# A weight quantiser split over two stages: pieces of six blocks instead of seven, the last eight blocks moved into later chunks, and one copy moved ahead of an exponential

## The chip, the cores and the metric

The kernel runs on one core of a Trainium2 chip. The metric is the device time of one execution in microseconds (us), from the first to the last instruction and what lies around them. Lower is better. The engines are TensorE (PE, matrix products and transposes), VectorE (DVE), ScalarE (ACT), GpSimd (POOL) and SyncE (SP, which issues transfers). Each runs its own instructions in order and waits on semaphores for the others.

## What is computed

The input is x, 64 sequences of 32 steps and 256 channels, and a condition of 64 x 256. Two layers follow each other:

```python
x = x + L0_attn(L0_cond(cond_2048, x, ...), Wq, Wk, Wv, Wo, gq, gk)          # L0_cond: a GRU over 32 steps
x = x + L0_ffn(L0_cond2(x, cond_2048[:, None, :], b), w_gate, w_up, w_down, ln_weight)   # causal convolution, ternary weights
x = x + L1_attn(L1_cond(x, cond_2048[:, None, :], ...), gamma, Wq, Wkv, Wo)  # small attention, then one with rotary positions
x = x + L1_ffn(L1_cond2(x, cond_2048[:, None, :]), w_fc, w_proj)             # convolution, relu squared
```

The two weights of the last line are quantised in the kernel, in blocks of 64. For each block 16 scales are tried, and the one with the smallest squared error is kept:

```python
base = jnp.maximum(amax, 1e-08) / QMAX              # QMAX = 15, amax over a block of 64
for s in SHRINKS:                                   # 16 factors, 0.4 to 1.0
    scale = base * s
    deq = jnp.clip(jnp.round(wb / scale), -QMAX, QMAX) * scale
    err = jnp.sum((deq - wb) ** 2, axis=-1, keepdims=True)
    # keep the scale of the smallest err
deq = jnp.clip(jnp.round(wb / best_scale), -QMAX, QMAX) * best_scale
```

With 128 partitions each partition holds 64 blocks, 4096 columns in all.

## The kernel before, in words

The order of the work is written by hand for each engine, and semaphores link the engines. It falls into three stages.

**The recurrence** (about 10 to 251 us). A Python loop over 32 steps. In a step PE adds the hidden part of the gates to the input part (L555), does the input part of the next step (L543, L546) and a share of the value projections of earlier states (L573), and turns the new state (L561). ACT takes the tanh of the gates (L1235) and of the candidate (L1239) and copies the turned state (L1245). DVE has five state instructions (L1975 to L1990). The quantiser lies between them. The 64 blocks of a partition are cut into eight pieces of seven blocks (448 columns), one per four steps, and eight blocks are left over. In each step one group of four scales is searched for one piece: ACT makes four scaled copies (`raised`, L1216), cuts the upper two (`from_top`, L1224) and squares (`squares`, L1229, L1230). DVE cuts the lower two (L1957), multiplies and adds four times (L1963, both in `round_off`) and sums the squares per block (L1949, `errors`). Once per piece DVE also finds the maxima (`piece_in`) and chooses and rounds (`piece_out`, spread over four steps), and POOL scales.

**Layer 0** (251 to about 790 us). Eight chunks of 256 tokens. Each chunk has projections, scores, softmax, outputs and, one and two chunks late, the convolution and the feed-forward part. A chunk from 2 on is called a tail chunk, as it also finishes the hidden layer of the chunk two before: `hidden` (L2118, the product of gate and up), `weigh` (L2126), `quantise_hidden` (L2131 to L2143), with ACT's `silu` (L1333) and `hidden_squares` (L1340), and POOL's two powers (L1746, L1750). PE's `gate_up` (L677) writes banks 6 and 7, and waits for `silu` and `hidden` of the previous gate to free them. The eight blocks that are left over are quantised here in chunks 0 and 1: `rest_group` (L1918 to L1923), ACT's `rest_squares` (L1287), `rest_errors` (L1929), `rest_out`. The quantised weights are stored to device memory and come back at the end of layer 0 in eight transfers.

**Layer 1** (about 790 to 1375 us). Nine passes of `chunk1`. A pass does the rotary attention of chunk i, the conditional attention of chunk i + 1 and the feed-forward part of earlier ones. PE turns the quantised weights in passes 0 and 1. Of the rotary part the prediction uses: ACT's exponentials of two halves (`rot_exps`, L1567), PE's outputs per half (`rot_outputs`, L965, four banks), ACT's copies of these (`keep_rot_outputs`, L1574), PE's projection (`rot_project`, L971), and in the conditional part ACT's spread of the probabilities (L1545) for PE's L920.

## Time and profile before

| | us |
|---|---|
| median of 3 runs | 1377.5 |
| lowest, highest | 1376.99, 1380.71 |
| the profiled execution, own time | 1377.21 |
| its span, first to last instruction | 1375.4 |

| engine | busy us | share of the span |
|---|---|---|
| PE, matrix products | 1290.9 | 94% |
| DVE | 1125.6 | 82% |
| ACT | 807.4 | 59% |
| POOL | 86.4 | 6% |

A share of busy time is an average over the three stages, which have different limits. So the rows below are from stretches: the busy time of each engine in a stretch, who waited for whom, and single instructions in order of time. In a timeline a row may join several equal instructions (x8 is eight of them). What stands in square brackets is the idle time of the engine before the row and what ended it. PE's instructions of full precision appear as two records each, and their ends are modelled. The second number behind a line in the busy table is the count of instructions.

### The profile page before, as it was taken

The numbers are of one execution on the slowest core, as the hardware profiler recorded it, in microseconds if no ns is written. First come the engines' busy times: TensorE is split into PE (matmuls) and PEld (weight loads), VectorE is DVE, ScalarE is ACT, GpSimd is POOL, SyncE is SP. The second block draws the span as 40 slices with busy tenths as digits, with TensorE's granted clock in tenths as the row PEclk, the third lists the DMA queues.
The fourth block names the chain that finished last, engine by engine and source line by source line (L and its number), as shares of the span: only waits on it lengthen the run. The fifth ranks groups of instructions, "written<-read, shape, count | busy, mean of one in ns | idle before, by whom it ended". The sixth has DMA issues, their size and how long they took to land.

```text
span 1375.4 us, 25080 instructions
## 1 busy us (share of the span) xinstructions
PE 1290.9 (94%) x9490; PEld 925.9 (67%) x9490; DVE 1125.6 (82%) x2903; ACT 807.4 (59%) x1550; POOL 86.4 (6%) x88
## 2 busy tenths in 40 slices
PE   5999999999999999999999848798999999999988
PEld 2444444578777888878787635476777777787867
DVE  4899999879989686877868889669797988888875
ACT  3999989875555565656565463535454545455323
POOL 0000000101020101010102000000000000000000
PEclk9999999999999999999999979899999999999999
DMA  9432333441111010102030420000000000000000
GB/s 377 123 77 62 77 92 75 151 129 32 40 39 47 32 48 31 48 31 76 3 117 24 157 77 1 24 16 8 9 24 1 24 1 24 1 16 9 8 1 24
DMA packets 26533, 74.18 MB, mean 54 GB/s; under 512 B 3992, under 2 KB 5156, under 8 KB 25136
## 3 DMA queue, kind: packets, MB, share of 16 engines
q1 hardware_dynamic: 25840, 71.62, 16.6%
q8 instruction: 75, 1.23, 0.4%
q10 hardware_dynamic: 576, 0.98, 0.2%
q14 instruction: 42, 0.34, 0.1%
HBM read 49.52 MB, written 23.07 MB: 53 GB/s over the span
## 4 chain that ended last, share of the span: by engine, by line
PE 68%; DVE 25%; ACT 4%; issue 2%; DMA 1%; SPq 0%; DVEq 0%; ACTq 0%
PE psum L619 14%; PE psum L971 9%; PE psum L728 8%; PE psum L940 7%; DVE work L1832 5%; DVE ffn_mem L1949 4%; PE psum L667 4%; PE psum L985 4%; DVE work L1963 3%; PE psum L1013 3%; PE psum L632 2%; PE psum L677 2%; PE psum L886 2%; PE psum L952 2%; PE psum L653 1%
## 5 line engine op out<-in xcount | busy, mean ns | idle before, releaser
L619 PE MATMUL psum<-h_all,w_big 128*128 128x256 f32 x1024 | 241.8, 384 | 1.1 <-ACT work L1283 1.0
L619 PEld LDWEIGHTS psum<-h_all,w_big 128*128 128x128 f32 x1024 | 188.4, 190 | 41.7 <-issue 16.0
L1832 DVE SCALAR_TENSOR_TENSOR work<-work,taps 128x248 f32<-128x248 f32 (+30 forms) x558 | 148.8, 351 | 0.0
L573 PE MATMUL psum<-w_big,h_all 128*64 128x512 f32 x512 | 124.8, 610 | 0.0
L940 PE MATMUL psum<-work,w_big 128*128 128x256 f32 x512 | 118.0, 379 | 0.5 <-DVE gru_mem L2383 0.5
L728 PE MATMUL psum<-w_big,gru_mem 128*128 128x256 f32 x512 | 113.6, 379 | 0.5 <-ACT gru_mem L1325 0.5
L971 PE MATMUL psum<-w_big 128*128 128x256 f32 x448 | 108.2, 393 | 5.9 <-ACT w_big L1574 5.9
L728 PEld LDWEIGHTS psum<-w_big,gru_mem 128*128 128x128 f32 x512 | 96.9, 190 | 14.7 <-ACT gru_mem L1325 0.6
L940 PEld LDWEIGHTS psum<-work,w_big 128*128 128x128 f32 x512 | 96.0, 190 | 13.5 <-DVE gru_mem L2383 0.9
L971 PEld LDWEIGHTS psum<-w_big 128*128 128x128 f32 x448 | 85.4, 195 | 25.8 <-ACT w_big L1574 8.5
L2381 DVE TENSOR_TENSOR gru_mem<-psum,trig 128x256 f32<-128x256 f32 x128 | 54.0, 422 | 40.9 <-PE psum L940 36.9
L1278 ACT ACTIVATE work<-psum,cols 128x512 f32<-128x512 f32 x64 | 44.0, 687 | 65.8 <-PE psum L619 65.8
L573 PEld LDWEIGHTS psum<-w_big,h_all 128*64 128x64 f32 x512 | 50.3, 202 | 42.4 <-issue 35.1
L1283 ACT ACTIVATE work<-psum 128x512 f32<-128x512 f32 x128 | 75.7, 591 | 0.0
L1832 DVE SCALAR_TENSOR_TENSOR h_all<-h_all,taps 128x248 f32<-128x248 f32 (+30 forms) x248 | 67.5, 348 | 0.0
L667 PE MATMUL psum<-probs_t,work 128*128 128x128 f32 x512 | 62.7, 279 | 0.9 <-ACT probs_t L1313 0.9
L667 PEld LDWEIGHTS psum<-probs_t,work 128*128 128x128 f32 x512 | 59.8, 192 | 4.8 <-ACT probs_t L1313 3.5
L2118 DVE SCALAR_TENSOR_TENSOR gru_mem<-psum,stats,work 128x512 f32<-128x512 f32 x28 | 20.9, 748 | 49.2 <-ACT work L1333 46.1
L1593 ACT ACTIVATE h_all<-psum 128x256 f32<-128x256 f32 x64 | 24.5, 383 | 62.4 <-PE psum L985 61.2
L1280 ACT ACTIVATE work<-psum 128x512 f32<-128x512 f32 x64 | 38.2, 597 | 37.3 <-PE psum L619 36.3
L1013 PE MATMUL psum<-ffn_mem,h_all 128*128 128x256 f32 x256 | 58.7, 383 | 0.0
L1013 PEld LDWEIGHTS psum<-ffn_mem,h_all 128*128 128x128 f32 x256 | 47.7, 190 | 12.7 <-issue 6.7
(324 smaller groups left out, 2537.5 us busy)
## 6 DMA issues: line engine op xcount, KB each, us to landing
value_rows<-w_emb SPq DMA_DIRECT2D x128, 128.0 KB, 2.3
work<-value_rows SPq DMA_DIRECT2D x16, 1024.0 KB, 6.0
w_big<-in_Wq SPq DMA_DIRECT2D x2, 2048.0 KB, 16.9
w_big<-in_Wo SPq DMA_DIRECT2D x2, 2048.0 KB, 21.4
out<-w_big SPq DMA_DIRECT2D x15, 256.0 KB, 2.1
x_res<-out SPq DMA_DIRECT2D x15, 256.0 KB, 2.8
w_big<-in_Wv SPq DMA_DIRECT2D x1, 2048.0 KB, 18.6
w_big<-in_Wk SPq DMA_DIRECT2D x1, 2048.0 KB, 23.1
```

The source lines that it names most:

```text
L573: mm = pe.matmul(bank(4 + n)[j * B:(j + 1) * B, :], h_all[:, k, :, 2 * pair + j], w_big[:, 2, k * H * HD + n * 512:k * H * HD + (n + 1) * ...
L619: mm = pe.matmul(bank(n % 2)[:, o * TA:(o + 1) * TA], w_big[:, s, k * H * HD + at:k * H * HD + at + HD], h_all[:, k, bass.ds(i * BA, BA), ...
L667: mm = pe.matmul(bank(4 + n % 2)[:, h * P:(h + 1) * P], v_tok[:, g, e * HD:(e + 1) * HD], probs_t[:, g * HU + e, :], start=True, stop=True)
L728: mm = pe.matmul(wo_out(c, g), o_t[:, h, g * P:(g + 1) * P], w_big[:, 3, h * D:(h + 1) * D], start=(h == 0), stop=(h == H - 1))
L940: mm = pe.matmul(bank((h + 2) % 4)[:, 0:TA], wq1[:, k, h * HD:(h + 1) * HD], xl_t[:, k, :], start=(k == 0), stop=(k == KD - 1))
L971: mm = pe.matmul(bank(wo1_bank(g))[:, 0:D], o1_of(c)[:, h, g * P:(g + 1) * P], wo1[:, h, :], start=(h == 0), stop=(h == H - 1), skip_group ...
L985: mm = pe.matmul(fc_out(c, f), fc_t[:, k, f * P:(f + 1) * P], ffn1(c)[2][:, k, :], start=(k == 0), stop=(k == KD - 1))
L1013: mm = pe.matmul(pj_out(c, g), h2_t[:, f, g * P:(g + 1) * P], proj_t[:, f, :], start=(f == 0), stop=(f == KF - 1))
L1283: act.activation(sq[:, pair % 2 * 2 + s, :], bank(n % 2), ACT.Square).then_inc(proj_kept.sem, 1)
L1832: ins = dve.scalar_tensor_tensor(dst[:, :, lag:], src[:, :, :T - lag], tap, dst[:, :, lag:], ALU.mult, ALU.add)
L1949: dve.tensor_reduce(err[:, g * GROUP:(g + 1) * GROUP, :].rearrange("p s b -> p (s b)"), blocks(w5_tmp[g].rearrange("p j n -> p (j n)")), A ...
L2381: dve.tensor_tensor(by_sequence(q_cos[:, h, :]), src, of_step(cos_q, BA), ALU.mult)
```

## The change

Three edits in one.

1. The pieces hold six blocks (384 columns) instead of seven. Eight pieces are 48 blocks. Sixteen blocks are left over: eight of them go the old way through chunks 0 and 1 (`rest`), the other eight, called `last`, form a new path.
2. The new path. SP loads the eight blocks after the sums for the film rows, into `w_emb`, where they stay: they are not stored and not loaded again. DVE starts them in chunk 2 (`last_begin`), and searches one group at the end of each of chunks 2 to 5 (`last_group`). ACT squares in the next chunk (`last_squares`), and DVE sums there inside `quantise_hidden`, between the maximum and the wait for POOL (`last_errors`). At the end of chunk 6 DVE chooses and rounds (`last_out`).
3. In two rotary passes, 1 and 7, ACT copies the outputs of the first half before it takes the exponential of the second half.

```diff
-PB = 7
+PB = 6
...
-RB = NBLK - PIECES * PB
+RB = (NBLK - PIECES * PB) // 2
 RC = RB * BLK
+LAST_AT = REST_AT + RC
...
+        last = w_emb[:, 2 * D:2 * D + RC]
+        last_abs = w_big[:, 2, 2560:2560 + RC]
+        last_tmp = w_big[:, 2, 0:GROUP * RC].rearrange("p (j n) -> p j n", j=GROUP)
...
             def last_chunk(i):
+                sp.wait_ge(rest_sum.sem, 2 * NG)
...
-                for n in range(PIECES):
+                for n in range(PIECES - 1):
                     sp.dma_start(w5_back[n], w5_dram[:, n * 512:(n + 1) * 512]).then_inc(w5_again, 16)
...
             chunk(0, False, False)
+            sp.wait_ge(film_sum.sem, 1)
+            sp.dma_start(last, io["w5"][:, LAST_AT:]).then_inc(w5_in, 16)
...
-                    pe.wait_ge(w5_again, 16 * PIECES)
+                    pe.wait_ge(w5_again, 16 * (PIECES - 1))
+                    pe.wait_ge(rest_done.sem, 2)
...
+            def last_squares(n):
+                act.wait_ge(rest_set.sem, NG + n + 2)
+                rest_sq.raised_by(act.activation(last_tmp, last_tmp, ACT.Square))
...
                 if tail:
                     hidden_squares(c - 1, 0)
+                    if i > 2:
+                        last_squares(i - 3)
...
+                unfilled = rot and (not late or not cond) and not begun
+                if unfilled:
+                    keep_rot_outputs(i, 0)
                 if rot:
                     rot_exps(i, 1)
...
-                if rot:
+                if rot and not unfilled:
                     keep_rot_outputs(i, 0)
...
+            def last_begin():
+                dve.wait_ge(w5_in, 32)
+                link(dve.tensor_reduce(rest_amax, blocks(last), AX.X, ALU.max, apply_absolute_value=True))
...
+                link(dve.tensor_tensor(blocks(last), blocks(last), per_block(rest_inv), ALU.mult))
+                link(dve.scalar_tensor_tensor(last_abs, last, -1.0, last, ALU.mult, ALU.max))
+
+            def last_group(g):
+                if g:
+                    dve.wait_ge(rest_sum.sem, NG + g)
+                for j in range(GROUP):
+                    ins = dve.tensor_scalar(last_tmp[:, j, :], last_abs, float(1.0 / SHRINKS[g * GROUP + j]), MAGIC,
+                                            ALU.mult, ALU.add)
+                link(ins)
+                link(dve.tensor_scalar(last_tmp, last_tmp, MAGIC + QMAX, MAGIC, ALU.min, ALU.subtract))
+                for j in range(GROUP):
+                    ins = dve.scalar_tensor_tensor(last_tmp[:, j, :], last_abs, -float(1.0 / SHRINKS[g * GROUP + j]),
+                                                   last_tmp[:, j, :], ALU.mult, ALU.add)
+                rest_set.raised_by(ins)
+
+            def last_errors(g):
+                dve.wait_ge(rest_sq.sem, NG + g + 1)
+                rest_sum.raised_by(dve.tensor_reduce(rest_err[:, g * GROUP:(g + 1) * GROUP, :].rearrange("p s b -> p (s b)"),
+                                                     blocks(last_tmp.rearrange("p j n -> p (j n)")), AX.X, ALU.add))
...
                 flink(dve.tensor_reduce(h_max, hid_w, AX.X, ALU.max, apply_absolute_value=True))
+                if meanwhile:
+                    meanwhile()
                 dve.wait_ge(hr_on.sem, GA * c + g + 1)
...
-                    quantise_hidden(c - 1, 0, tail_link)
+                    quantise_hidden(c - 1, 0, tail_link, lambda: last_errors(i - 3) if i > 2 else last_begin())
...
+                if tail:
+                    if i - 2 < NG:
+                        last_group(i - 2)
+                    else:
+                        last_out()
```

`last_out` (not shown) is `rest_out` on the new names, with the final multiplication on DVE instead of POOL: eleven instructions.

How the instructions stand, in three places. First DVE in the recurrence, before, from the last state instruction of a step to the next step's first ones (the names are those of the areas; L1949 sums, L1957 cuts, L1963 multiplies and adds):

```order
L1990 SCALAR_TENSOR_TENSOR gru_mem<-gru_mem,probs_t 128x128
L1949 TENSOR_REDUCE ffn_mem<-work 128x28
L1957 TENSOR_SCALAR work<-work 128x896
L1963 SCALAR_TENSOR_TENSOR work<-probs_t,work 128x448 x4
L1877 TENSOR_TENSOR ffn_mem<-ffn_mem,shrink_tab 128x112
L1879 TENSOR_REDUCE ffn_mem<-ffn_mem 128x7
```

and now:

```order
L2049 SCALAR_TENSOR_TENSOR gru_mem<-gru_mem,probs_t 128x128
L2008 TENSOR_REDUCE ffn_mem<-work 128x24
L2016 TENSOR_SCALAR work<-work 128x768
L2022 SCALAR_TENSOR_TENSOR work<-probs_t,work 128x384 x4
L1894 TENSOR_TENSOR ffn_mem<-ffn_mem,shrink_tab 128x96
L1896 TENSOR_REDUCE ffn_mem<-ffn_mem 128x6
```

The order is the same, and each instruction is a seventh shorter.

Second, DVE from the end of a layer-0 chunk (L2106, the rounded input of the feed-forward part) into the next, at the boundary of chunks 2 and 3, before:

```order
L2106 TENSOR_SCALAR work<-work 128x512
L2118 SCALAR_TENSOR_TENSOR gru_mem<-psum,stats,work 128x512 x2
L2126 TENSOR_TENSOR gru_mem<-gru_mem,ffn_mem 128x1024
L2131 TENSOR_SCALAR stats<-stats 128x1
L2133 TENSOR_REDUCE stats<-gru_mem 128x1
L2136 TENSOR_SCALAR stats<-stats 128x1
```

and now:

```order
L2165 TENSOR_SCALAR work<-work 128x512
L1976 TENSOR_SCALAR w_big<-w_big 128x512 x4
L1979 TENSOR_SCALAR w_big<-w_big 128x2048
L1981 SCALAR_TENSOR_TENSOR w_big<-w_big 128x512 x4
L2177 SCALAR_TENSOR_TENSOR gru_mem<-psum,stats,work 128x512 x2
L2185 TENSOR_TENSOR gru_mem<-gru_mem,ffn_mem 128x1024
L2190 TENSOR_SCALAR stats<-stats 128x1
L2192 TENSOR_REDUCE stats<-gru_mem 128x1
L1987 TENSOR_REDUCE v<-w_big 128x32
L2197 TENSOR_SCALAR stats<-stats 128x1
```

The group (L1976 to L1981) stands before the first hidden product, and the error sum (L1987) between the maximum and the scalar instruction that waits for POOL.

Third, ACT in the last rotary pass, before (the two exponentials L1567, both halves' copies L1574, then the turned rows L1581 and the feed-forward part):

```order
L1595 ACTIVATE h_all<-h_all 128x256
L1567 ACTIVATE work<-work 128x512 x2
L1574 ACTIVATE w_big<-psum 128x16x32 x8
L1581 ACTIVATE work<-psum 128x512
L1593 ACTIVATE h_all<-psum 128x256
```

and now:

```order
L1609 ACTIVATE h_all<-h_all 128x256
L1581 ACTIVATE work<-work 128x512
L1588 ACTIVATE w_big<-psum 128x16x32 x4
L1581 ACTIVATE work<-work 128x512
L1588 ACTIVATE w_big<-psum 128x16x32 x4
L1595 ACTIVATE work<-psum 128x512
```

The first four copies moved ahead of the second exponential.

## Rows read from the trace of the kernel before

**Rows 1.** Busy time by stretch (length, then busy us by engine): recurrence, chunk.

```profile
54.06:248.60 194.54, 180.85 (x877) 80.33 (x875) 183.34 (x372) 175.81 (x316) 12.31 (x13) 1.00 0.33 78
520.20:585.30 65.10, 65.10 (x648) 52.44 (x641) 50.74 (x134) 38.28 (x66) 6.48 (x3) 1.00 0.13 41
```

**Rows 2.** Waits, 54 to 248 us: who, for whom, total us, times, longest.

```profile
PE psum L561 <- DVE gru_mem L1990: 13.6, 25, 0.9
```

**Rows 3.** Timeline of PE, recurrence: start us, length us, line, instruction, idle before.

```profile
32.96 0.33 PE L561 MATMUL psum<-ident,gru_mem 128*128 128x128 f32 x1
39.91 0.33 PE L561 MATMUL psum<-ident,gru_mem 128*128 128x128 f32 x1
...
54.20 0.33 PE L561 MATMUL psum<-ident,gru_mem 128*128 128x128 f32 x1
...
243.33 0.33 PE L561 MATMUL psum<-ident,gru_mem 128*128 128x128 f32 x1 [0.95 <-DVE gru_mem L1990]
250.76 0.48 PE L561 MATMUL psum<-ident,gru_mem 128*128 128x128 f32 x1 [2.16 <-DVE gru_mem L1990]
```

**Rows 4.** DVE lines of the quantiser: ns min/median/max, first and last start us.

```profile
L1949 DVE TENSOR_REDUCE ffn_mem<-work x24: 2009/2010/2014, 39.6 to 265.7; 128x28 f32<-128x1792 f32 x24
L1929 DVE TENSOR_REDUCE v<-w_big x4: 2276/2276/2287, 295.7 to 338.4; 128x32 f32<-128x2048 f32 x4
L1963 DVE SCALAR_TENSOR_TENSOR work<-probs_t,work x48: 617/619/627, 56.6 to 257.1; 128x448 f32<-128x448 f32 x48
L1923 DVE SCALAR_TENSOR_TENSOR w_big<-work,w_big x16: 684/685/693, 281.8 to 330.1; 128x512 f32<-128x512 f32 x16
L1957 DVE TENSOR_SCALAR work<-work x24: 615/617/621, 24.8 to 253.4; 128x896 f32<-128x896 f32 x24
```

**Rows 5.** ACT's pass over the upper half of a group, the same view.

```profile
L1224 ACT ACTIVATE work<-work,top_col x24: 1027/1033/1058, 21.5 to 254.3; 128x896 f32<-128x896 f32 x24
```

**Rows 6.** Timeline of DVE: a group's first instruction, and the one behind it.

```profile
279.08 1.43 DVE L1918 TENSOR_SCALAR w_big<-work 128x512 f32<-128x512 f32 x4
284.22 0.18 DVE L1838 TENSOR_SCALAR stats<-stats 128x32 int32<-128x32 int32 x1
```

**Rows 7.** Timeline of DVE in a layer-0 chunk, from its first hidden product.

```profile
586.90 0.75 DVE L2118 SCALAR_TENSOR_TENSOR gru_mem<-psum,stats,work 128x512 f32<-128x512 f32 x1 [5.69 <-ACT work L1333]
595.40 0.21 DVE L2136 TENSOR_SCALAR stats<-stats 128x1 f32<-128x1 f32 x1 [2.18 <-POOL stats L1750]
613.65 0.74 DVE L1828 TENSOR_SCALAR work<-work,taps,cols 128x256 f32<-128x256 f32 x2 [1.02 <-ACT work L1350]
```

**Rows 8.** ACT: end of that chunk's hidden squares; line L1287 by itself.

```profile
591.71 0.18 ACT L1340 ACTIVATION_READ_ACCUMULATOR gru_mem<-gru_mem 128x1 f32 x1
L1287 ACT ACTIVATE w_big<-w_big x4: 1902/1910/1912, 286.1 to 330.8; 128x2048 f32<-128x2048 f32 x4
```

**Rows 9.** Timeline of the same chunk: DVE's third product, PE's fourth gate.

```profile
597.62 0.75 DVE L2118 SCALAR_TENSOR_TENSOR gru_mem<-psum,stats,work 128x512 f32<-128x512 f32 x1
598.48 1.03 PE L677 MATMUL psum<-ffn_mem,work 128*128 128x512 bf16 x4
```

**Rows 10.** Timeline of the same chunk: POOL's power and DVE's L2126.

```profile
589.36 5.43 POOL L1746 TENSOR_TENSOR stats<-stats,minus_half 128x32 f32<-128x32 f32 x1 [44.65 <-ACT stats L1301]
590.75 1.22 DVE L2126 TENSOR_TENSOR gru_mem<-gru_mem,ffn_mem 128x1024 f32<-128x1024 f32 x1
```

**Rows 11.** Timeline of PE and ACT in the last rotary chunk.

```profile
1317.66 1.64 PE L965 MATMUL psum<-work,v 32*128 32x512 f32 x8
1322.24 5.41 PE L971 MATMUL psum<-w_big 128*128 128x256 f32 x16 [2.93 <-ACT w_big L1574]
1320.15 2.04 ACT L1574 ACTIVATE w_big<-psum 128x512 f32<-128x512 f32 x4
```

**Rows 12.** Timeline of ACT and PE in rotary chunk 1.

```profile
945.56 2.54 ACT L1545 ACTIVATE probs_t<-work 32x512 f32<-32x512 f32 x4 [2.89 <-DVE work L2348]
949.13 1.08 PE L920 MATMUL psum<-probs_t,work 128*32 128x128 f32 x32
```

More of the change, by code:

```diff
@@ L497, in _ @@
             chunk(0, False, False)
+            sp.wait_ge(film_sum.sem, 1)
+            sp.dma_start(last, io["w5"][:, LAST_AT:]).then_inc(w5_in, 16)
             chunk(1, False, True)
             sp.wait_ge(rest_done.sem, 1)
-            sp.dma_start(w5_dram[:, REST_AT:], rest).then_inc(w5_out, 16)
-            with sp.Fori(0, NA - 3) as last:
-                chunk(last + 2, True, True)
+            sp.dma_start(w5_dram[:, REST_AT:LAST_AT], rest).then_inc(w5_out, 16)
+            with sp.Fori(0, NA - 3) as later:
+                chunk(later + 2, True, True)
             last_chunk(NA - 1)
@@ L1737, in _ @@
             pool.wait_ge(in_step.sem, in_step.at(PIECES + 1, 0))
-            rest_based.raised_by(pool.tensor_tensor(blocks(rest), blocks(w5[:, REST_AT:]), per_block(rest_inv), ALU.mult))
+            rest_based.raised_by(pool.tensor_tensor(blocks(rest), blocks(w5[:, REST_AT:LAST_AT]), per_block(rest_inv), ALU.mult))
             times_scale(PIECES - 2)
@@ L1788, in _ @@
             rest_done.raised_by(pool.tensor_tensor(blocks(rest), blocks(rest), per_block(rest_scale), ALU.mult))
-            with pool.Fori(0, NA - 3) as last:
-                chunk(last + 2, True, True)
+            with pool.Fori(0, NA - 3) as later:
+                chunk(later + 2, True, True)
             head_rms(UNITS - 2)
@@ L1900, in slink @@
                     link(ins, in_step, PIECES)
-                slink(dve.tensor_reduce(rest_amax, blocks(w5[:, REST_AT:]), AX.X, ALU.max, apply_absolute_value=True))
+                slink(dve.tensor_reduce(rest_amax, blocks(w5[:, REST_AT:LAST_AT]), AX.X, ALU.max, apply_absolute_value=True))
                 slink(dve.tensor_scalar(rest_base, rest_amax, 1e-8, None, ALU.max))
@@ L1944, in rest_out @@
                 rest_set.raised_by(dve.tensor_scalar(rest, rest, MAGIC, MAGIC, ALU.add, ALU.subtract))
+            def last_begin():
+                dve.wait_ge(w5_in, 32)
+                link(dve.tensor_reduce(rest_amax, blocks(last), AX.X, ALU.max, apply_absolute_value=True))
+                link(dve.tensor_scalar(rest_base, rest_amax, 1e-8, None, ALU.max))
+                link(dve.tensor_scalar(rest_base, rest_base, 1.0 / QMAX, None, ALU.mult))
+                link(dve.reciprocal(rest_inv, rest_base))
+                link(dve.tensor_tensor(blocks(last), blocks(last), per_block(rest_inv), ALU.mult))
+                link(dve.scalar_tensor_tensor(last_abs, last, -1.0, last, ALU.mult, ALU.max))
@@ new lines, in last_errors, with last_out @@
+            def last_errors(g):
+                dve.wait_ge(rest_sq.sem, NG + g + 1)
+                rest_sum.raised_by(dve.tensor_reduce(rest_err[:, g * GROUP:(g + 1) * GROUP, :].rearrange("p s b -> p (s b)"),
+                                                     blocks(last_tmp.rearrange("p j n -> p (j n)")), AX.X, ALU.add))
+            def last_out():
+                dve.wait_ge(rest_sum.sem, 2 * NG)
+                link(dve.tensor_tensor(rest_err, rest_err, shrinks_sq.unsqueeze(2).broadcast_to([P, NS, RB]), ALU.mult))
+                link(dve.tensor_reduce(rest_best, rest_err.rearrange("p s b -> p b s"), AX.X, ALU.min))
+                link(dve.tensor_tensor(rest_pick, rest_err, rest_best.unsqueeze(1).broadcast_to([P, NS, RB]), ALU.is_gt))
+                link(dve.scalar_tensor_tensor(rest_pick, rest_pick, 2.0, shrinks.unsqueeze(2).broadcast_to([P, NS, RB]),
+                                              ALU.mult, ALU.add))
+                link(dve.tensor_reduce(rest_shr, rest_pick.rearrange("p s b -> p b s"), AX.X, ALU.min))
+                link(dve.reciprocal(rest_ishr, rest_shr))
+                link(dve.tensor_tensor(rest_scale, rest_shr, rest_base, ALU.mult))
+                link(dve.tensor_tensor(blocks(last), blocks(last), per_block(rest_ishr), ALU.mult))
+                link(dve.tensor_scalar(last, last, float(QMAX), -float(QMAX), ALU.min, ALU.max))
+                link(dve.tensor_scalar(last, last, MAGIC, MAGIC, ALU.add, ALU.subtract))
+                rest_done.raised_by(dve.tensor_tensor(blocks(last), blocks(last), per_block(rest_scale), ALU.mult))
@@ L2126, in weigh, with quantise_hidden @@
                 dve.tensor_tensor(hid_w, hid, ln_row, ALU.mult).then_inc(hidw_on.sem, 1)
-            def quantise_hidden(c, g, flink):
+            def quantise_hidden(c, g, flink, meanwhile=None):
                 _, hid_w, hid_q, _, _ = hid_bufs(c)
```

2 lines of the change are left out of this document (1 added, 1 removed).

## The prediction, made before the changed kernel was run

> **What bounds the kernel now.** I read the page first, then the busy table of two stretches, as the page's shares are averages over stages. The table splits them: in the recurrence (54 to 249 us) PE, DVE and ACT are all near 90% or more, DVE highest with 183.34 of 194.54 us; in a layer-0 chunk (65.1 us) PE is busy 65.10 of 65.10 us and DVE only 50.74 [rows 1]. So the two places want opposite things: DVE work is dear in the recurrence and has 14.4 us of room in a chunk. What counts there is where the room lies.
>
> Third view, the waits of the recurrence: PE stood before the turn of the new state (L561) for 13.6 us in 25 times, each time for the last DVE instruction of the step, L1990 [rows 2]. The starts of L561 in the timeline give the pitch: from 54.20 to 243.33 us are 25 steps, 189.13 us, 7.565 us each. The same PE work ran from 32.96 to 39.91 us without a wait: 6.95 us [rows 3]. DVE sets the pitch, but PE is only 0.6 us per step behind it.
>
> **The quantiser's pieces.** Each of the 32 steps holds one group of the search. Its DVE part loses 64 of 448 columns in every instruction. The costs come from the same operations at two widths [rows 4]: the error sum took 2010 ns for 1792 columns and 2276 for 2048, 1.04 ns per column, so 256 fewer columns save 0.265 us. The four multiply-adds took 619 ns at 448 and 685 at 512, 66 ns per 64 columns, so 4 x 66 = 0.26 us. The cut-off (617 ns at 896) runs at about twice that rate: 128 columns, 0.07 us. The work on a piece (maximum, final rounding, once in four steps) has five 448-wide instructions, 65 or 33 ns less each, about 0.06 us per step. The sum is 0.65 us: DVE alone would allow 7.565 - 0.65 = 6.91 us.
>
> ACT loses work too. At 0.76 ns per column (1910 ns at 2048 [rows 8] against 1033 at 896 [rows 5]) four raised copies save 4 x 49 ns and three 896-wide passes 3 x 97 ns: 0.49 us, from 175.81 / 194.54 x 7.565 = 6.84 us busy per step [rows 1] to 6.35. ACT does not become the limit.
>
> What is late next is PE. Its bound of 6.95 us sits 0.04 above DVE's 6.91. DVE's steps are unequal (243.33 to 250.76 is 7.43, the mean 7.565 [rows 3]), but it can run ahead in a short step, as nothing but the state ties it to PE, so the long step is absorbed. The gain is 25 x (7.565 - 6.95) = 15.4 us if the clean step repeats, and 13.6 us if only the waits go [rows 2, 3]. I take 14.5. After the last step PE waits 2.16 us [rows 3]; it issues less there, and its DVE path shortens by the same 0.65 us: 0.8 with the lead that DVE then has (bounds 0 and 2.16). Start-up and hand-over to the projections hold some ACT-bound waits of the same copies; from some 0.4 us less ACT work in one step I estimate 0.7 for both ends together (bounds 0 and 2). Part a: -16.0 us.
>
> The transfer of the input weights is 256 KB shorter at the start and comes later as a load of its own; the store and the reload of the eight last blocks go. All lie beside computation: SP has nothing urgent behind the new wait for the film sums, since it stands after the value load that needs later outputs, and the wait in the last chunk is met early in chunk 6.
>
> **The eight blocks in chunks 2 to 6.** Three additions per chunk.
>
> A group of the search goes to the end of chunks 2 to 5. The same group for the first eight blocks ran from 279.08 to 284.22 us: 5.14 us [rows 6]. It falls into the idle stretch before the first hidden product, 5.69 us long, ended by ACT L1333 [rows 7]. 0.55 us remain: cost 0. If this cover were gone, its length would stand in full before L2118, whose product frees the bank that PE's next gate needs. The final choice in chunk 6 has eleven instructions: four 512 wide, of at most 0.69 us each as L1923 [rows 4], and seven on 128 columns or fewer, at most 0.4 us by estimate. That is under 5.6 us, in the same gap: 0.
>
> The error sum goes between the maximum and the wait for POOL, 2.18 us of idle [rows 7]. It needs ACT's square. ACT is free at 591.9 us (its accumulator read starts at 591.71 and lasts 0.18), and the square of 2048 columns took 1910 ns for the first eight blocks [rows 8]: done at 593.8. DVE's sum of 2.28 us then ends near 595.95, and L2136 begins there and not at 595.40: +0.55 us. Queued behind it on DVE is the third hidden product, L2118 at 597.62 for 0.75 us, then ending at 598.9. PE starts gate 3 at 598.48 [rows 9] and needs that bank about 0.43 us later, for its second half: a wait of 0 to 0.15 us. The rest of the chain is absorbed before the convolution, where DVE idles 1.0 us [rows 7]. Chunk 2 has instead the beginning (three instructions of 512 columns, some 0.69 us each, and three small ones, 0.2 by estimate), 2.7 us in the 2.18 us gap: +0.5 us, within the same slack. I take +0.3 us for all five chunks; bounds 0 and 5 x 0.55 = 2.75.
>
> The trace shows POOL's power running from 589.36 for 5.43 us, and DVE's two-operand L2126 starting inside it at 590.75 and lasting 1.22 us for 1024 columns [rows 10], just what L1963 and L1923 give without POOL (1.03 ns per column and 0.16 fixed, 1.21 us [rows 4]). So the two-operand instructions of the beginning should not wait for POOL. The Trainium skill (SBUF — State Buffer, "Summary: rules for kernel authors") speaks against that: a DVE operation with two SBUF inputs and a GpSimd one that reads SBUF exclude each other, and the second waits. By that rule the beginning would end about 0.8 us later, and part b would be 1.1 instead of 0.3; the row disagrees, so the sum goes by the row.
>
> **The rotary copies.** In the last rotary chunk PE starts the outputs at 1317.66 us; the copies run from 1320.15 for 2.04 us, behind the second exponential, and PE waits 2.93 us for them until 1322.24. Put first, they can start when the first output is done. I take 1.15 us after its start, 1318.8, within bounds of 0.3 and 1.64 (the length of the PE row): copies done at 1320.85, and PE goes on 1.3 us earlier (0.9 to 2.2). The exponential is then about 1.2 us later; what needs it, PE's second outputs, comes only after PE's projection of 5.41 us, with over 3 us of room [rows 11].
>
> In chunk 1 the same exchange starts PE's projection about 0.9 us earlier, but the exponential slips behind the copies, by 1.5 us (estimated from the 1.2 of the last pass, where DVE's scores are ready later), and with it the DVE chain to ACT's spread of the conditional probabilities (945.56, 2.54 us long). That then ends at 949.6; PE wants it at about 948.2 and began at 949.13 before [rows 12]. Net +0.5 us (bounds -0.9 and +1.5). Part c: -1.3 + 0.5 = -0.8 us.
>
> **The sum** against the profiled execution, 1377.2 us (its span is 1375.4): -16.0 + 0.3 - 0.8 = -16.5, so 1360.7. The median of the runs is 0.3 above that execution: 1361.0 us.
>
> **Rivals.**
> 1. PE's true floor is higher. The three engines hand the state around, and with PE, DVE and ACT within 0.7 us of each other each wait of one falls on the next. For it: DVE's 6.91 and PE's 6.95 almost meet, and some steps have 0.5 us more ACT or DVE work. Against it: the loop of the state alone is much shorter than the pitch. If half of part a's 14.5 us stays, the time is 1361.0 + 7.2 = 1368.2 us.
> 2. The DVE work of the chunks reaches PE. The added work is 4 x 5.14 + 4 x 2.28 + 2.7 + some 4.5 (the final choice) = 36.9 us. PE has no idle in a chunk [rows 1], so every microsecond by which DVE delays a bank is lost. The place is L2118: if the group and the sum come in front of it by a full delay, the price is 36.9 us, 0.3 of it in the sum already, and the time 1361.0 + 36.6 = 1397.6 us. It turns the gain of 16.8 us into a loss once 46% of the added work is uncovered. Against it: by length, all but 1 us per chunk has a gap.
> 3. DVE is no limit in the recurrence after all, so that the change doesn't do there what it says, and only part c and the ends are left: 1375 us. Rows 2 name DVE 25 times, so little speaks for it.
>
> **Chances.** Forecast (1357 to 1365): 0.66. Rival 1 (1365 to 1372): 0.22. Rival 2: 0.06, of which 0.04 end slower than 1381.6 and 0.02 in between. Rival 3: 0.03, within the bound in half of it and just beyond in the other. A gain above the sum (PE's pitch below 6.95, or more at the ends), under 1357: 0.03. The measurement of this kernel tells 0.3%, 4.1 us, from no change. Faster: 0.66 + 0.22 + 0.03 + half of rival 3 and a little of rival 2 = 0.93; same 0.03; slower 0.04. The range 1357 to 1370 leaves out rivals 2 and 3, the 0.03 below and about 0.05 of rival 1: 0.17.
>
> **What the changed profile would show.** L561 at a pitch of 6.95 to 7.02 us with waits of under 0.1 us, DVE with waits before L1975 or for ACT instead. DVE's idle before the first hidden product down from 5.69 to about 0.5 us; the error sum starting about 3.0 us after its chunk's first L1340 and PE's row of a chunk still 65.1 us. In the last rotary chunk a PE wait of 1.6 instead of 2.93 us. The forecast is wrong if the pitch is above 7.15 or if a chunk lasts over 65.6 us.

## The result

| | before | after |
|---|---|---|
| median, us | 1378.01 (4 runs, 1376.99 to 1380.71) | 1361.33 (4 runs, 1359.24 to 1362.78) |
| span of the profiled execution | 1375.4 | 1359.6 |

The ratio is 0.9875, 95% interval 0.9855 to 0.9894. The prediction was 1361.0.

The lines named here moved down by 7 to 61: L561 is now L568 (the state's turn), L555 L562, L573 L580, L677 L684, L965 and L971 are L972 and L978, L1574 is L1588, L1545 L1559, L1949 L2008, L1957 L2016, L1963 L2022, L2118 L2177, L2136 L2197. L1224 is L1232.

**The recurrence.** Busy time by stretch, as in [rows 1]: the 25 steps from 54.16 us, and one layer-0 chunk.

```profile
54.16:228.40 174.24, 174.10 (x853) 77.90 (x851) 160.87 (x364) 158.11 (x307) 11.00 (x13) 1.00 0.34 81
504.30:569.50 65.20, 65.20 (x641) 52.42 (x640) 57.99 (x145) 40.07 (x67) 6.48 (x3) 1.00 0.14 42
```

PE is busy for the whole of the recurrence's stretch, and DVE is below it. In the chunk DVE went from 50.74 to 57.99 us, and PE stays full. PE's waits for the state, 54 to 237 us, against the 25 of [rows 2]:

```profile
PE psum L568 <- DVE gru_mem L2049: 1.5, 1, 1.5
```

The timeline of PE at the turns, answering to [rows 3]:

```profile
54.30 0.33 PE L568 MATMUL psum<-ident,gru_mem 128*128 128x128 f32 x1
...
228.30 0.33 PE L568 MATMUL psum<-ident,gru_mem 128*128 128x128 f32 x1
235.05 0.33 PE L568 MATMUL psum<-ident,gru_mem 128*128 128x128 f32 x1 [1.48 <-DVE gru_mem L2049]
```

From 54.30 to 228.30 us are 25 steps of 6.96 us, with no wait at the turn. The only wait left stands before the last turn. The DVE and ACT lines at the new widths, against [rows 4, 5]:

```profile
L2008 DVE TENSOR_REDUCE ffn_mem<-work x24: 1741/1745/1754, 39.6 to 248.4; 128x24 f32<-128x1536 f32 x24
L2022 DVE SCALAR_TENSOR_TENSOR work<-probs_t,work x48: 550/552/560, 56.1 to 240.6; 128x384 f32<-128x384 f32 x48
L2016 DVE TENSOR_SCALAR work<-work x24: 548/550/555, 23.9 to 237.4; 128x768 f32<-128x768 f32 x24
L1232 ACT ACTIVATE work<-work,top_col x24: 919/923/937, 20.7 to 238.2; 128x768 f32<-128x768 f32 x24
```

**A layer-0 chunk.** DVE and PE in chunk 3, against [rows 7 to 9]:

```profile
440.55 0.75 DVE L2177 SCALAR_TENSOR_TENSOR gru_mem<-psum,stats,work 128x512 f32<-128x512 f32 x1 [0.55 <-ACT work L1345]
447.45 2.29 DVE L1987 TENSOR_REDUCE v<-w_big 128x32 f32<-128x2048 f32 x1 [0.58 <-ACT w_big L1299]
449.66 0.20 DVE L2197 TENSOR_SCALAR stats<-stats 128x1 f32<-128x1 f32 x1
```

```profile
452.13 1.14 PE L684 MATMUL psum<-ffn_mem,work 128*128 128x512 bf16 x4
```

The gap of 5.69 us is filled down to 0.55. DVE waits 0.58 us for the square (L1299), and the scalar instruction behind the error sum starts 0.6 us late (0.61 against the kernel before, with the rows of PE laid on each other). PE's row of four gate products at 452.13 takes 1.14 us where 1.03 is usual: 0.1 us is what reaches it.

**The last rotary pass**, PE and ACT, against [rows 11]:

```profile
1304.43 1.64 PE L972 MATMUL psum<-work,v 32*128 32x512 f32 x8
1307.77 3.72 PE L978 MATMUL psum<-w_big 128*128 128x256 f32 x16 [1.70 <-ACT w_big L1588]
```

```profile
1305.65 2.06 ACT L1588 ACTIVATE w_big<-psum 128x512 f32<-128x512 f32 x4 [3.83 <-PE psum L972]
```

The wait is 1.70 us instead of 2.93, and the projection behind it takes 3.72 us instead of 5.41.

**Where the 15.8 us of the two spans are.** The same row of PE was found in both traces, and its times subtracted. The stretches between those in the table differ by under 0.1 us.

| stretch | after less before, us | predicted |
|---|---|---|
| start-up, to the turn at 54.20 | +0.10 | |
| 25 steps | -15.13 | -14.5 |
| last step | -0.68 | -0.8 |
| hand-over to layer 0 | -0.62 | -0.7, start-up included |
| chunks 2 to 6 | +0.61 | +0.3 |
| layer 1, pass 0 | +1.87 | 0 |
| pass 1 | +0.62 | +0.5 |
| last pass and end | -2.58 | -1.3 |

The 1.87 us of pass 0 were in no term. PE's first projection there, before and after:

```profile
882.29 3.72 PE L971 MATMUL psum<-w_big,gru_mem 128*128 128x256 f32 x16
```

```profile
866.69 5.48 PE L978 MATMUL psum<-w_big,gru_mem 128*128 128x256 f32 x16
```

Sixteen equal records, 3.72 and 5.48 us. Two more stretches of the table hold the clock. From the first turn of the state to the sixth (54.20 us in the kernel before) the first profile took 36.81 us, against 36.18 before, but at a mean granted clock of 0.91 against 0.95. And in the kernel before the last turn took 0.48 us where 0.33 is usual [rows 3]: the mean granted clock from there to 254 us was 0.50, and the changed kernel's profile has 1.00 behind its last turn. Both come up again below. So the experiments had three things to settle: what bounds the recurrence now, what the path of the last eight blocks costs, and what the clock does in layer 1.

### The profile page after: what moved, and what is told of

It reads as the page before. It is cut to its first block, busy times and chain, and to the rows that moved or that the text cites. A ratio compares the mean times of both kernels' runs of the same rounds, so it can differ in the third digit from the quotient of the medians.

```text
span 1359.6 us, 25143 instructions
## 1 busy us (share of the span) xinstructions
PE 1288.5 (95%) x9490; PEld 926.3 (68%) x9490; DVE 1139.4 (84%) x2960; ACT 798.7 (59%) x1554; POOL 85.0 (6%) x88
## 3 DMA queue, kind: packets, MB, share of 16 engines
q8 instruction: 75, 1.23, 0.4%
## 4 chain that ended last, share of the span: by engine, by line
PE 80%; DVE 14%; ACT 3%; issue 1%; DMA 1%; SPq 0%; DVEq 0%; ACTq 0%
PE psum L626 14%; PE psum L735 8%; PE psum L580 7%; PE psum L978 7%; PE psum L947 7%; DVE work L1849 5%; PE psum L674 4%; PE psum L992 4%; PE psum L1020 3%; PE psum L553 3%; PE psum L562 3%; PE psum L639 2%; PE psum L684 2%; PE psum L893 2%; PE psum L959 2%
## 5 line engine op out<-in xcount | busy, mean ns | idle before, releaser
L580 PE MATMUL psum<-w_big,h_all 128*64 128x512 f32 x512 | 124.0, 606 | 0.0
L978 PE MATMUL psum<-w_big 128*128 128x256 f32 x448 | 106.5, 389 | 3.8 <-ACT w_big L1588 3.8
L978 PEld LDWEIGHTS psum<-w_big 128*128 128x128 f32 x448 | 84.4, 193 | 23.0 <-ACT w_big L1588 6.4
L580 PEld LDWEIGHTS psum<-w_big,h_all 128*64 128x64 f32 x512 | 50.3, 203 | 42.7 <-issue 35.5
L1763 POOL TENSOR_TENSOR stats<-stats,minus_half 128x32 f32<-128x32 f32 x7 | 38.4, 5482 | 280.9 <-ACT stats L1313 280.9
```

The source lines that it names most:

```text
L580: mm = pe.matmul(bank(4 + n)[j * B:(j + 1) * B, :], h_all[:, k, :, 2 * pair + j], w_big[:, 2, k * H * HD + n * 512:k * H * HD + (n + 1) * ...
L978: mm = pe.matmul(bank(wo1_bank(g))[:, 0:D], o1_of(c)[:, h, g * P:(g + 1) * P], wo1[:, h, :], start=(h == 0), stop=(h == H - 1), skip_group ...
```

## The experiments

Experiments 1 to 4 ran beside a kernel before of 1380.2 us, 5 to 8 beside 1378.66, 9 to 12 beside 1378.46, so ratios are compared, not times. Experiments 9 and 10 have one execution each (1355.57 and 1352.48 us), so only their rows are read. Where an interval is some 0.4% wide, a difference of 1 or 2 us is read in the trace, from the same rows of PE.

### 1 to 3: the rotary copies

1: `unfilled = False`. 2: `unfilled = rot and not cond and not begun`. 3: the third edit alone, on the kernel before.

> The changed kernel with its third edit undone: both rotary passes take the second exponential ahead of the first copies again. Theory A (the clock is part of it; read from the two traces): in the last pass the edit took 1.23 us off PE's wait and the projection behind it ran in 3.72 instead of 5.41 us, as the granted clock did not fall; pass 1 lost 0.62. Undoing it costs +2.58 - 0.62 = +2.0 us: 1363.3, and the last pass's projection takes 5.41 us again. Theory B (the prediction's term c, waits only): +0.8 us, 1362.1, and 5.41 against 3.72 us is chance, so that the projection may take 3.72 us here as well.

> The changed kernel with the early copies in the last pass alone; pass 1 as before the change. Theory A: pass 1 gives its 0.62 us back (no PE wait of 1.41 us for the spread of the conditional probabilities), the last pass keeps its 2.58: 1360.7 us. Rival: the projection of pass 1 starts 0.85 us later and the gain is lost there, the spread being late either way: 1361.3 to 1361.6.

> The kernel before with the third edit alone. If the parts add up: 1378.0 - 2.0 = 1376.0 us, with PE's wait in the last pass 1.70 us and the projection behind it 3.72 us (the clock is kept). By waits alone: 1377.2, projection 5.41 us.

Measured: 1366.19 us, ratio 0.9883 (0.9864 to 0.9902); 1363.01 us, 0.9865 (0.9844 to 0.9886); 1378.98 us, 0.9987 (0.9976 to 0.9998). Timeline of PE in the last pass, first experiment 1 (copies late), then 2 (copies early):

```profile
1310.18 6.71 PE L978 MATMUL psum<-w_big 128*128 128x256 f32 x16 [2.94 <-ACT w_big L1588]
```

```profile
1308.02 5.41 PE L978 MATMUL psum<-w_big 128*128 128x256 f32 x16 [1.69 <-ACT w_big L1588]
```

The ratios are too near each other to tell the theories apart: that of experiment 3 is 1.8 us below its kernel before, where 2.0 and 0.8 were expected, with an interval of 0.3 to 3.3. So the rows decide. Waits went as expected (2.94 and 1.69 us). The projection did not: 6.71 us in 1, and 5.41 in 2 although its copies are early. Experiment 3 had 3.72 us in the last pass (2.93 us gained up to the end of the projection, 0.35 of it lost again behind it) but in pass 1 this:

```profile
942.84 3.72 PE L971 MATMUL psum<-w_big 128*128 128x256 f32 x16 [2.08 <-ACT w_big L1574]
950.73 1.42 PE L920 MATMUL psum<-probs_t,work 128*32 128x128 f32 x32 [3.10 <-ACT probs_t L1545]
952.08 5.02 PE L971 MATMUL psum<-w_big 128*128 128x256 f32 x16
```

The projection (942.84) ran fast there, but PE then stood 3.10 us for the spread, and the next two rows ran slowly: pass 1 lost 2.26 us in all, and not 0.6. Neither theory holds: the time behind a wait isn't fixed.

### 4: without the new path

```diff
-                    if i > 2:
-                        last_squares(i - 3)
-                    quantise_hidden(c - 1, 0, tail_link, lambda: last_errors(i - 3) if i > 2 else last_begin())
+                    quantise_hidden(c - 1, 0, tail_link)
-                if tail:
-                    if i - 2 < NG:
-                        last_group(i - 2)
-                    else:
-                        last_out()
```

> The changed kernel without the new path: the eight last blocks are loaded but not quantised (that part of the computation is left out). What chunks 2 to 6 pay for it: by the landmarks of the two traces 0.1 us per chunk and 0.2 in chunk 2, 0.6 us in all: 1360.7. The prediction's term was 0.3: 1361.0. Rival (contention or bank delays that the landmarks hide, or the low clock in pass 0 of layer 1 being a consequence of the path's waits there): 2 us or more, 1359.3 or less, with pass 0 at the speed of before (projection of pass 0 3.72 instead of 5.48 us).

Measured: 1361.06 us, 0.9861 (0.9841 to 0.9882). Against the changed kernel's first profile its rows of PE stand at +0.25 us after chunk 1 and at -0.38 after chunk 6: the path costs 0.63 us, 0.2 in chunk 2 and 0.11 in each of the others. The rival falls: pass 0's projection took 3.72 us here, but also in experiments 5, 6, 8, 9, 11 and 12, which have the path.

### 5, 9 and 10: what bounds the recurrence

5: one multiply-add of four left out (`for j in range(1, GROUP)` in `round_off`). 9: in every second tile of the values the product of the second half of the channels is left out. 10: both.

> The changed kernel with three instead of four multiply-adds per group of the search in the recurrence (one of four is left out of the computation): 0.55 us less DVE work per step, DVE alone would allow about 6.4 us. Theory (PE sets the pitch): the pitch stays at 6.95 to 6.96 us, the time within 1 us of 1361.3. Rival 1 of the prediction (the engines hand the state around and each wait of one falls on the next): the pitch falls by 0.2 us or more, 5 us or more in the time.

> The last try left out one of a pair of products whose two halves of 64 columns share a time slot, so PE lost next to nothing (the step's row of four records went from 1.14 to 1.12 us and the one behind it from 1.46 to 1.86). Here both halves of the pair go: four records fewer per step, about 1.0 us (part of the values isn't computed). Only the pitch of the recurrence is read. PE alone would allow about 5.97 us. By the prediction's count DVE binds at 6.91 us: pitch 6.90 to 6.95. Rival: DVE had more room than counted: pitch below 6.85.

> The same with one multiply-add of each group left out on DVE as well. DVE's count is then 6.91 - 0.55 = 6.36 us, PE's 5.97, ACT's 6.35 (busy time of before less the prediction's 0.49). If the three bounds stand for themselves, the pitch is 6.36 to 6.45 us. Rival 1 of the prediction (waits of one engine fall on the next): 6.6 us or more.

The turns 25 steps apart, in experiments 5, 9 and 10 in this order:

```profile
53.73 0.33 PE L568 MATMUL psum<-ident,gru_mem 128*128 128x128 f32 x1
...
227.53 0.33 PE L568 MATMUL psum<-ident,gru_mem 128*128 128x128 f32 x1
```

```profile
52.19 0.33 PE L568 MATMUL psum<-ident,gru_mem 128*128 128x128 f32 x1
...
224.52 0.33 PE L568 MATMUL psum<-ident,gru_mem 128*128 128x128 f32 x1 [0.63 <-DVE gru_mem L2049]
```

```profile
52.48 0.33 PE L568 MATMUL psum<-ident,gru_mem 128*128 128x128 f32 x1
...
220.42 0.33 PE L568 MATMUL psum<-ident,gru_mem 128*128 128x128 f32 x1
```

5: 6.95 us per step (1360.22 us, ratio 0.9864, 0.9847 to 0.9881). Less DVE work brings nothing: PE is the bound. 9: 6.89 us per step. PE was busy for 154.07 of 170 us (55 to 225 us), 6.25 us per step, so its work fell by 0.7 us, and the pitch by 0.06 only. PE's idle time is 11.5 us behind the turn, for ACT's copy of the turned state (L1253), and 3.9 us ahead of it, for DVE. So without DVE PE would step at about 6.73 us, and DVE holds it at 6.89; the prediction's count for DVE was 6.91. 10: 6.72 us, where 6.36 to 6.45 were expected of three bounds that stand for themselves. Busy time of 10, 55 to 225 us, in the columns of the first table, then PE's waits there, and PE's timeline from one turn to the next:

```profile
55.00:225.00 170.00, 156.72 (x762) 68.84 (x761) 150.93 (x344) 160.20 (x310) 11.00 (x13) 1.00 0.36 86
```

```profile
PE psum L562 <- ACT h_all L1253: 12.0, 25, 0.5
PE psum L568 <- DVE gru_mem L2049: 1.3, 6, 0.2
```

```profile
106.25 0.33 PE L568 MATMUL psum<-ident,gru_mem 128*128 128x128 f32 x1
107.06 1.57 PE L562 MATMUL psum<-gru_mem,h_all 128*64 128x384 f32 x8 [0.47 <-ACT h_all L1253]
...
112.89 0.33 PE L568 MATMUL psum<-ident,gru_mem 128*128 128x128 f32 x1
```

ACT is busy 94% of the time, PE 92%, DVE 89%, and none is full. But PE's 156.72 us of work and its two waits, 12.0 and 1.3 us, make up the whole 170 us: PE still sets the pitch. The products that were left out are those that PE does between the turn (L568) and the first product that needs its copy (L562). They had covered ACT's copy, and without them PE stands 0.47 us for it in every step. So the edit took 0.7 us of work off PE and gave 0.47 us back as a wait, and PE's own bound in 9 and 10 is about 6.7 us and not 5.97. That explains the 0.3 us between the expectation and 6.72; DVE delays PE by 0.05 us per step. What experiment 10 can't tell is whether the pitch would have come down to DVE's 6.36 us with a faster PE. In the changed kernel PE has no such wait.

### 6 and 7: an experiment that missed

In every second tile one product of 64 output columns was left out: 6 from the changed kernel, 7 from the kernel before.

> The changed kernel with one of the eight value products of a step left out of the recurrence (part of the values isn't computed): 0.46 us less PE work per step. PE alone would allow 6.49 us. By the prediction's count DVE then binds at 6.91 us, so the pitch falls by only 0.04 us and the time by 1 us. Rival: DVE's bound is lower than counted, or there is none, and the pitch falls towards 6.5 us, 11 us in all.

> The kernel before with the same value product left out: PE 0.46 us less per step. Theory (DVE set the pitch before): pitch 7.57 us and time 1378.0 unchanged, PE's waits longer by 0.46 us each. Rival 3 of the prediction (DVE was no limit): pitch 7.1 us, time 1366.

Measured: 1368.1 us, 0.9927 (0.9902 to 0.9953), and 1386.22 us, 1.0058 (1.0037 to 1.0079). The pitch hardly moved in either (6.94 and 7.56 us), which says nothing, as PE's work hardly fell. PE in experiment 6, one step:

```profile
102.73 0.33 PE L568 MATMUL psum<-ident,gru_mem 128*128 128x128 f32 x1
102.99 1.13 PE L580 MATMUL psum<-w_big,h_all 128*64 128x512 f32 x2
103.54 1.86 PE L562 MATMUL psum<-gru_mem,h_all 128*64 128x384 f32 x8
```

The same two rows in the changed kernel:

```profile
103.22 1.15 PE L580 MATMUL psum<-w_big,h_all 128*64 128x512 f32 x4
104.20 1.46 PE L562 MATMUL psum<-gru_mem,h_all 128*64 128x384 f32 x8
```

The four hidden products (L562) take 1.86 us behind two records where they took 1.46 behind four, and end 2.4 us behind the first record in both. The two halves of 64 columns run beside each other, so half a pair saves nothing. The Trainium skill says that the array can be split into tiles that are independent of each other (TensorEngine Tiling (Array Packing), "Overview"); these rows agree. Both kernels lost some 7 us elsewhere, in chunks 2 to 6. PE's waits of experiment 6 there, 300 to 760 us:

```profile
PE psum L626 <- issue: 2.4, 2, 1.9
PE psum L660 <- issue: 2.3, 4, 0.8
```

The changed kernel has no wait of this kind there. "Issue" means that nothing in the profile held PE. The program of PE is 30 instructions shorter ahead of these places; experiment 9, with 60 fewer, has no such loss. Why it comes is open.

### 8: the group without its gap

```diff
                     quantise_hidden(c - 1, 0, tail_link, lambda: last_errors(i - 3) if i > 2 else last_begin())
+                    if i - 2 < NG:
+                        last_group(i - 2)
...
-                if tail:
-                    if i - 2 < NG:
-                        last_group(i - 2)
-                    else:
-                        last_out()
+                if tail and i - 2 >= NG:
+                    last_out()
```

> The changed kernel with the group of the search moved from the end of its chunk to behind the error sum's place in the hidden quantiser of the same chunk, ahead of the third hidden product: 5.14 us of DVE work without a gap, the same count of instructions. Theory (the prediction's cover, rival 2's price): each of four chunks pays 5.14 less about 0.4 us of slack, 4.7 us; 1361.3 + 19 = 1380 us. Rival (the place doesn't matter, as DVE has 14 us of room in a chunk and catches up): under 3 us, 1364 or less.

Measured: 1390.33 us, 1.0086 (1.0068 to 1.0104): 29 us slower than the changed kernel. By the rows of PE the four chunks lost 7.65, 7.15, 6.73 and 6.62 us, more than the 5.14 us that the group lasts. PE in chunk 3, then the second of the two rows in the changed kernel, then the busy table of that row's stretch:

```profile
463.97 1.03 PE L684 MATMUL psum<-ffn_mem,work 128*128 128x512 bf16 x2 [5.07 <-DVE gru_mem L2177]
464.79 8.62 PE L735 MATMUL psum<-w_big,gru_mem 128*128 128x256 f32 x32
```

```profile
442.63 7.07 PE L735 MATMUL psum<-w_big,gru_mem 128*128 128x256 f32 x32
```

```profile
464.79:473.25 8.46, 8.46 (x34) 7.09 (x32) 8.14 (x13) 2.98 (x4) 0.00 (x0) 0.82 0.00 0
```

PE waited 5.07 us for the hidden product, and the 32 records behind it took 8.62 us instead of 7.07, at a mean granted clock of 0.82 instead of 1.00. So this wait of 5.07 us cost 1.5 us more than itself in the row behind it alone.

### 11: the changed kernel again

> The changed kernel again, unaltered. Theory (TensorE's granted clock behind short waits in layer 1 differs from execution to execution): pass 0's projection, 5.48 us in the first profile, may take 3.72 us as in six of the nine other profiles, and pass 1 and the last pass may differ as well; time 1359 to 1364 us. Rival (each kernel has its own fixed pattern): 5.48, 5.41 and 3.72 us in passes 0, 1 and 7 again.

Measured: 1360.83 us, 0.9881 (0.9865 to 0.9898). PE in passes 0 and 1:

```profile
865.92 3.72 PE L978 MATMUL psum<-w_big,gru_mem 128*128 128x256 f32 x16
...
925.49 3.72 PE L978 MATMUL psum<-w_big 128*128 128x256 f32 x16 [2.08 <-ACT w_big L1588]
933.38 1.60 PE L927 MATMUL psum<-probs_t,work 128*32 128x128 f32 x32 [3.10 <-ACT probs_t L1559]
934.91 4.84 PE L978 MATMUL psum<-w_big 128*128 128x256 f32 x16
```

The same program, and pass 0's projection takes 3.72 us and not 5.48. In pass 1 the projection ran fast and the rows behind the wait slowly. The rival falls. (The expectation counts six fast ones among the nine other profiles; they were seven.) All fourteen profiles, by the length of the first projection (16 records):

| pass | copies | full clock, 3.72 us | lower clock |
|---|---|---|---|
| 0 | not edited | 10: before, 3 to 9, 11, 12 | 4: after, 1, 2, 10 (5.48 to 5.80) |
| 1 | late, wait 2.93 | none | 5: before, 1, 2, 7, 12 (5.23 to 5.41) |
| 1 | early, wait 2.08 | 7: 3, 4, 5, 6, 8, 9, 11 | 2: after, 10 (5.41) |
| last | late, wait 2.93 | none | 3: before, 1, 7 (5.37 to 6.71) |
| last | early, wait 1.70 | 9: after, 3 to 6, 8 to 11 | 2: 2, 12 (5.41) |

Behind a wait of 2.93 us the clock was at its lower level in all eight cases, behind one of 2.08 in two of nine, behind one of 1.70 in two of eleven. Where it held behind the 2.08 us of pass 1 it was low behind the next wait, of 3.10 us, in all seven cases. What decides between the two the rows do not show.

### 12: a candidate

```diff
-                rest_sq.raised_by(act.activation(last_tmp, last_tmp, ACT.Square))
+                for h in range(2):
+                    part = last_tmp[:, 2 * h:2 * h + 2, :]
+                    rest_sq.raised_by(act.activation(part, part, ACT.Square))
```

The error sum is cut in the same way, and `unfilled` is that of experiment 2.

> A candidate: the changed kernel with the early copies in the last pass alone, and with the square and the error sum of the last eight blocks cut in two halves of 1024 columns each, so that DVE sums the first while ACT squares the second. Theory: the second half's sum ends about 0.1 us before POOL's power and the 0.1 us per chunk vanishes in chunks 3 to 6 (-0.4 us); pass 1 gives back 0.6 to 0.8 us: 1.1 us below the unaltered changed kernel of the same call. That is less than the measurement tells; the landmarks of the trace must show it. Rival: the halves cost as much as they save (two fixed costs), and the chunk stays 0.1 us longer.

Measured: 1359.61 us, 0.9865 (0.9849 to 0.9882), 1.2 us below the changed kernel that ran beside it (experiment 11), which the intervals do not tell apart. DVE and then PE in chunk 3:

```profile
446.58 2.35 DVE L1991 TENSOR_REDUCE v<-w_big 128x16 f32<-128x1024 f32 x2
448.85 0.20 DVE L2202 TENSOR_SCALAR stats<-stats 128x1 f32<-128x1 f32 x1
```

```profile
451.81 1.03 PE L684 MATMUL psum<-ffn_mem,work 128*128 128x512 bf16 x4
```

DVE sums without a wait, and the scalar instruction starts at 448.85 us, 0.48 us earlier than in the changed kernel once the 0.33 is taken off by which this execution is ahead. PE's row is back at 1.03 us. Over chunks 3 to 6 PE gains 0.43 us, as expected: the halves hold. Pass 1, from the start of the outputs to the conditional projection, takes 15.16 us, against 15.79 in the first profile of the changed kernel and 17.42 in experiment 11. But the last pass's projection ran at the lower clock (5.41 us), as in experiment 2, which gives 1.69 us back. Another 1.47 us went in chunk 7, where this execution has the lower clock (0.50 from 754 to 757 us) and the changed kernel's two profiles do not. Both kernels with the early copies in the last pass alone had the slow projection there, and none of the nine profiles with them in both passes. Whether that is chance is open.

## Why the prediction was right

**The recurrence** carried the forecast and held. The unit costs came out: the error sum 1745 ns (2010 less 265 predicted, exactly that), each multiply-add 552 (619 less 66 is 553), the cut 550 (617 less 67 is 550). ACT's pass fell by 110 ns where 97 were counted: that is 0.86 ns per column, and the 0.76 of the prediction came from two different operations. PE's floor, read from one clean step of before, was the pitch of 25 steps (6.96 us), and experiments 5 and 9 show that the two bounds lie where the count put them: PE at 6.95, DVE at 6.89 against 6.91. I had taken 14.5 between 13.6 and 15.4; 15.13 is near the upper end, so the cautious discount of 0.9 us was not needed. Rival 3 is excluded as far as the pitch goes: it fell by 0.61 us with the work of DVE and ACT. That it was DVE's share is read from the waits and not from a run, as experiment 7 missed: in the kernel before PE and ACT stood 13.6 and 18.2 us for DVE in the 25 steps, and DVE 4.9 us for ACT. Rival 1 is excluded for this kernel: PE has no wait in the 25 steps, and less work on DVE changed nothing (experiment 5). Experiment 10 was to look for it further down and met another limit, a wait that its own edit uncovered. The last step gave 0.68 of the 0.8.

**Start-up and hand-over** were sized at 0.7 us together, and the first profile shows 0.52. At equal clocks it is more. The turn of 54.30 us stood between 52.78 and 54.59 in seven executions of kernels that are the same up to there. From the first turn to the sixth five of them took 35.35 to 35.63 us, at a mean granted clock of 0.95, and two (the first profile and experiment 12) 36.81 and 36.90 us at 0.91; the kernel before and experiment 3, with the old recurrence, took 36.18 and 36.10 us at 0.95. So the narrower pieces save 0.5 to 0.8 us there, which the first profile hid behind the clock. Of the 0.62 us of the hand-over 0.14 are the clock: experiment 3, without the lower level there, took 6.46 us from the last turn to the seventeenth record of L619, and the kernel before 6.60. The term was too small, and that it fits the profile is luck.

**The eight blocks.** The gap carried the group in all four chunks at no cost that shows, and experiment 8 shows what the gap was worth: 7 us per chunk. Rival 2's mechanism was right, its price too low, as the clock adds to each wait. The delay of L2136 by 0.55 us was seen (0.6), and what reached PE, bounded by 0 and 0.15 us, was 0.10 to 0.11 in chunks 3 to 6; 0.2 in chunk 2. The total was 0.61 to 0.63 instead of the 0.3 taken: I had set the middle of the bounds too low. In chunk 2 stands the beginning: its two-operand instructions on DVE, and POOL's two powers beside them:

```profile
382.99 0.69 DVE L1969 TENSOR_TENSOR w_emb<-w_emb,stats 128x512 f32<-128x512 f32 x1
383.72 0.69 DVE L1970 SCALAR_TENSOR_TENSOR w_big<-w_emb 128x512 f32<-128x512 f32 x1
377.72 5.43 POOL L1763 TENSOR_TENSOR stats<-stats,minus_half 128x32 f32<-128x32 f32 x1 [0.49 <-ACT stats L1313]
383.11 0.97 POOL L1767 TENSOR_TENSOR stats<-stats,minus_half 128x1 f32<-128x1 f32 x1
```

DVE's two take the length that they have without POOL (685 ns in [rows 4]). POOL's second power, which starts while the first of them runs, takes 0.97 us, as in all ten profiles that have the beginning (0.97 to 0.98); in the other chunks it takes 0.54, and in experiment 4, without the beginning, 0.55 in chunk 2 too. DVE's scalar instruction starts at 384.44 us behind L1970 in any case, so PE loses nothing by it. So the rule of the Trainium skill that the prediction weighed (SBUF — State Buffer, "Summary: rules for kernel authors") shows here after all, though on POOL's side: the second to start waits, 0.43 us. The prediction's row was the long power, under which DVE runs on freely, and it does so here as well (L2185, with two operands, starts inside it at 379.11 us and takes 1.23 us); what was concluded for DVE held, and of a wait on POOL's side the prediction had nothing.

**The rotary copies** hold in the term of the wait (-1.23 predicted as -1.3, copies 1.22 us behind the start of the outputs, 1.15 taken). What the prediction missed is the clock: in [rows 11] it had the row L971 with 5.41 us, and 3.72 is what sixteen such records take at the full clock. The busy table of that row, before and after:

```profile
1322.24:1327.58 5.34, 5.34 (x17) 4.11 (x17) 5.34 (x17) 0.00 (x0) 0.00 (x0) 0.68 0.00 0
```

```profile
1307.77:1311.42 3.65, 3.65 (x16) 2.96 (x17) 3.06 (x7) 0.46 (x1) 0.00 (x0) 1.00 0.00 0
```

0.68 and 1.00. So in this execution the row behind the shorter wait took 1.69 us less as well, and 0.35 was lost at the end. 1.00 is the level of 2.4 GHz, and 0.68 is a mean over stretches at it and at 1.2 GHz; before both rows PE had waited, 2.93 and 1.70 us. The Trainium skill describes these two levels, the lower one after idle time (TensorE: Matmul & The Clock Gate, "What's actually happening"); the rows agree in direction, and the table of experiment 11 shows that the same wait can go either way. In pass 1 the net price was 0.62 us as predicted (0.5), but only because pass 1's projection was slow in that profile; in seven of nine it was not, and the price was then about 2.3 us. So the agreement of this term is luck.

**The offset.** The mechanisms were right, but that the total is right to 0.3 us is in part luck, as its errors cancel. The last pass gave 1.28 us more than was counted, for the clock, and the 25 steps 0.63 us more; pass 0 took 1.87 us, for the clock too, and the other terms together some 0.7 us. That leaves 0.7 us, and the median of the runs lies 0.1 below the profiled execution, where 0.3 above was taken. The 1.87 us are no fixed effect of the change: the same program was without them in experiment 11. Whether the change makes them more frequent is open (4 of 11 profiles with the new recurrence had them, none of 3 with the old one).

## What to carry to other kernels

Find the second bound before moving work off the first: here DVE had 0.65 us per step to lose and only 0.61 of it counted, because PE's clean step (one pair of rows without a wait) was 6.95 us. Work moved into a gap costs what the gap's end delays, and the same work outside the gap can cost more than its length, as the clock was lower behind PE's longer wait (experiment 8). Before work is left out to find a bound, look what it covers: behind the turn it was a copy on another engine, and 0.47 us of the 0.7 came back as a wait (experiments 9 and 10). When a PE row behind a wait is longer than the same records elsewhere, shortening the wait may give back that difference too, but not in every execution, so don't count it as certain.

## What was not expected of the hardware

- The granted clock behind the same wait differs between executions of one program: 5.48 or 3.72 us for sixteen records of pass 0 (0.67 and 1.00 of full speed).
- POOL's power of one column takes longer beside a two-operand DVE instruction that started before it (0.97 for 0.54 us, in ten of ten profiles), while DVE's two-operand instruction starts unhindered under POOL's long power.
- Leaving out one of two 64-column halves saved PE nothing (1.86 behind two records for 1.46 behind four).
- Two kernels with a slightly shorter PE program before layer 0 stood for "issue" in chunks 2 to 6 and lost some 7 us there; a third, shorter still, didn't.
- PE can be 92% busy and still be the engine that sets the pitch, while ACT is 94% busy and doesn't: its work and a wait of 0.47 us per step for one copy fill the 6.72 us (experiment 10).
